# Combined weight quarters on GpSimd's own queue, ScalarE's queue first at the start, and S3/S4 formed where they are used

## The reference

```
c   = conv1d(x, weight[128, 32, 9], 4 groups, padding 4) + cond @ c_weight^T + bias     # [32, 128, 2048]
y   = c @ W[2048, 2048] + ffn_bias
d   = B_eff @ (A_eff @ c) + B_shared @ (A_shared @ c)    # rank 32 each; A_eff, B_eff mixed by gate per 4 samples
out = x + y + d
```

## Time and profile before

| | |
|---|---|
| median of 3 runs | 1772.81 us (1769.04 to 1773.53) |
| profiled execution | 1771.03 us, span 1769.2 us |
| busy: PE / PE weight loads / DVE / ACT / POOL | 1732.3 / 1482.9 / 996.0 / 668.0 / 184.7 us |
| DMA | 411.22 MB, mean 232 GB/s, nearly all on SP's queue |
| mean granted TensorE clock | 0.987 of full speed |

### The profile page before, as it was taken

How to read it: one execution, slowest core, us unless ns; L and a number is a source line. 1 busy time by engine, 2 the same in 40 slices (tenths; PEclk the granted TensorE clock), 3 DMA queues, 4 the chain that set the end, 5 groups by cost and what they waited for, 6 DMA issues and landing times.

```text
span 1769.2 us, 21998 instructions
## 1 busy us (share of the span) xinstructions
PE 1732.3 (98%) x8710; PEld 1482.9 (84%) x8710; DVE 996.0 (56%) x1183; ACT 668.0 (38%) x841; POOL 184.7 (10%) x70
## 2 busy tenths in 40 slices
PE   7999998999999998999999999999999999999998
PEld 7988887888788887999999888888888888888887
DVE  7566554552544489999997423345555544553332
ACT  6556655663322266565553212132322311121110
POOL 0023344000000012332223100000000000000000
PEclk9799999999999999999999999999999999999999
DMA  8668898643765646877776554457767798886654
GB/s 244 164 221 282 314 313 288 217 133 106 234 235 201 221 167 249 305 278 273 276 265 229 202 183 176 173 189 246 235 215 228 248 341 312 300 284 214 193 196 147
DMA packets 182287, 411.22 MB, mean 232 GB/s; under 512 B 58724, under 2 KB 94404, under 8 KB 177544
## 3 DMA queue, kind: packets, MB, share of 16 engines
q1 hardware_dynamic: 182040, 408.76, 68.2%
q10 hardware_dynamic: 144, 1.05, 0.2%
HBM read 263.72 MB, written 146.03 MB: 232 GB/s over the span
## 4 chain that ended last, share of the span: by engine, by line
PE 83%; DMA 7%; DVE 4%; POOL 3%; SPq 1%; issue 1%; ACT 1%; DVEq 0%; ACTq 0%
PE acc L1288 62%; PE cps L1204 13%; PE acc L1220 3%; DMA T<-g 3%; PE cps L1236 3%; DMA g<-in_L_ffn_kernel 2%; DVE x_q L893 1%; PE acc L1267 1%; POOL g L654 1%; POOL g L652 1%; POOL g L651 1%; POOL g L656 1%; DMA mixed_B<-b_raw 1%; DVE x_lo L900 1%; PE cps L1249 1%
## 5 line engine op out<-in xcount | busy, mean ns | idle before, releaser
L1288 PE MATMUL acc<-w_hi,y_t 128*128 128x512 f32 x3584 | 996.1, 392 | 0.0
L1288 PEld LDWEIGHTS acc<-w_hi,y_t 128*128 128x128 f32 x3584 | 667.2, 189 | 135.3 <-issue 1.6
L1288 PE MATMUL acc<-w_lo,y_t 128*128 128x512 f32 x1792 | 554.2, 390 | 0.0
L1288 PEld LDWEIGHTS acc<-w_lo,y_t 128*128 128x128 f32 x1792 | 337.6, 188 | 71.7
L684 ACT COPY x_q<-x_raw 32x512 f32<-32x512 f32 x248 | 268.7, 1084 | 50.1 <-DVE x_lo L900 38.6
L1204 PE MATMUL cps<-cw_hi,x_hi 128*128 128x384 f32 (+2 forms) x768 | 232.7, 303 | 10.5 <-DVE x_lo L900 6.9
L1204 PE MATMUL cps<-cw_lo,x_hi 128*128 128x384 f32 (+2 forms) x768 | 232.2, 302 | 0.0
L1204 PE MATMUL cps<-cw_hi,x_lo 128*128 128x384 f32 (+2 forms) x768 | 231.5, 301 | 0.0
L710 ACT CAST y_t<-g 128x1024 fp32r<-128x1024 f32 x96 | 101.1, 1053 | 335.0 <-PE acc L1288 309.3
L986 DVE TENSOR_TENSOR g<-acc,g 128x1024 f32<-128x1024 f32 x96 | 117.1, 1221 | 171.7 <-PE acc L1220 117.0
L947 DVE TENSOR_TENSOR y_t<-g,y_t 128x1024 fp32r<-128x1024 f32 x96 | 119.5, 1245 | 129.3 <-ACT y_t L710 129.2
(11 more groups left out here) (100 smaller groups left out, 1076.4 us busy)
## 6 DMA issues: line engine op xcount, KB each, us to landing
g<-U SPq DMA_DIRECT2D x80, 512.0 KB, 5.8
g<-A SPq DMA_DIRECT2D x64, 512.0 KB, 5.1
g<-in_x SPq DMA_DIRECT2D x64, 512.0 KB, 6.2
out<-g SPq DMA_DIRECT2D x64, 512.0 KB, 3.4
x_raw<-in_x SPq DMA_DIRECT2D x31, 1024.0 KB, 6.8
A<-g SPq DMA_DIRECT2D x48, 512.0 KB, 5.8
S<-g SPq DMA_DIRECT2D x48, 512.0 KB, 3.0
U<-g SPq DMA_DIRECT2D x48, 512.0 KB, 3.8
```

The source lines that it names most:

```text
L1288: ins = T.matmul(acc[:, b, m, :], y_buf[b][:, c, part, :], wt[:, k % SLOTS, m * 512:(m + 1) * 512], start=(c == 0 and part == 0 and wt is ...
```

## The change

- Forming: the four loads and four stores of each quarter chunk are issued by GpSimd itself, between its operations; SP's `forming` goes. SP still waits for all of it (`form_out`) before `load_y(16)`.
- Start: conv weights, x[0] and the first four B11 chunks are issued by ScalarE, in this order. VectorE forms cw_lo before the ctx copies and ctx_sum after `split_0(2)`; TensorE's ctx matmul stands behind conv(0)'s first group.
- Bias rows: split by `bias_hi` / `bias_lo` in iterations 15 and 80 and no longer in `b_split`.
- S3, S4: GpSimd forms nothing in phase 2. Phase 2 stores A21, A22, S1, S2 and loads A11 (double buffered); `difference(u)` on VectorE forms S3 = A11 - A21 and S4 = A12 - S2 in phases 3 and 6 from two loads (`load_y`, `load_other` into x_raw), one unit ahead.

```diff
@@ SP
-            def load_forming(j): ...
-            def store_formed(j): ...
-            def forming(u): ...
@@ load_y
-                elif f == 3:
-                    sp.wait_ge(s_out[1], 16 * (NP if p < 2 else p + 1))
-                    if p < 2:
-                        sp.wait_ge(s_out[2], 16 * NP)
+                elif f == 3 and p < 2:
+                    sp.wait_ge(s2_ready, NP - 1 + p)
-                src = {1: A12_d, 3: S3_d, 4: A22_d, 5: S1_d, 6: S4_d}[f]
+                src = {1: A12_d, 3: A11_d, 4: A22_d, 5: S1_d, 6: A12_d}[f]
+            def load_other(u):
+                f, p, b = u // NP, u % NP, u % 2
+                if f == 3:
+                    sp.wait_ge(yc_out[0], 16 * (NP + p + 1))
...
+                if diff_index(u) >= 2:
+                    sp.wait_ge(diff_ready, diff_index(u) - 1)
+                sp.dma_start(other[b], (A21_d if f == 3 else S2_d)[p]).then_inc(other_in[b], 16)
@@ load_sums -> load_a11
-                for i, src in enumerate((A11_d, A12_d)):
-                    if p == 0:
-                        sp.wait_ge(yc_out[i], 16 * NP)
-                        sp.wait_ge(y_lo_ready, 2 * NP)
-                    else:
-                        sp.wait_ge(s_out[1 + i], 16 * p)
-                    sp.dma_start(g[:, 2 + i], src[p]).then_inc(a1_in[i], 16)
+                if p < 2:
+                    sp.wait_ge(yc_out[0], 16 * NP)
+                    sp.wait_ge(y_lo_ready, 2 * NP - 1 + p)
+                else:
+                    sp.wait_ge(s2_ready, p - 1)
+                sp.dma_start(a11_buf[p % 2], A11_d[p]).then_inc(a1_in[p % 2], 16)
@@ GpSimd
             for j in range(NCH):
+                if j == 0:
+                    pool.wait_ge(la_used, RK)
+                else:
+                    pool.wait_ge(form_out, 64 * j)
+                for i, quarter in enumerate((B11, B12, B21, B22)):
+                    V.dma_start(g[:, 2 + i], quarter[j]).then_inc(form_in, 16)
                 pool.wait_ge(form_in, 64 * (j + 1))
                 V.tensor_tensor(g[:, 5], g[:, 5], g[:, 3], ALU.subtract).then_inc(form_done, 1)
                 V.tensor_tensor(g[:, 3], g[:, 3], g[:, 2], ALU.subtract).then_inc(form_done, 1)
                 pool.wait_ge(form_done, 4 * j + 2)
+                V.dma_start(T7_d[j], g[:, 5]).then_inc(form_out, 16)
                 V.tensor_tensor(g[:, 2], g[:, 5], g[:, 2], ALU.add).then_inc(form_done, 1)
+                V.dma_start(T5_d[j], g[:, 3]).then_inc(form_out, 16)
                 pool.wait_ge(form_done, 4 * j + 3)
+                V.dma_start(T6_d[j], g[:, 2]).then_inc(form_out, 16)
                 V.tensor_tensor(g[:, 4], g[:, 4], g[:, 2], ALU.subtract).then_inc(form_done, 1)
-            for p in range(NP):
-                pool.wait_ge(y_evac, 4 * (NP + p + 1))
-                pool.wait_ge(s2_ready, p + 1)
-                V.tensor_tensor(g[:, 2], g[:, 2], g[:, 0], ALU.subtract).then_inc(s3_ready, 1)
-                pool.wait_ge(a1_in[1], 16 * (p + 1))
-                V.tensor_tensor(g[:, 3], g[:, 3], s2_buf, ALU.subtract).then_inc(s4_ready, 1)
+                pool.wait_ge(form_done, 4 * j + 4)
+                V.dma_start(T4_d[j], g[:, 4]).then_inc(form_out, 16)
@@ ScalarE
+            act.dma_start(b_raw[:, 0:GC * TAPS], conv_w.rearrange("o i k -> o (i k)")).then_inc(conv_w_in, 16)
             act.dma_start(x_raw[:], x[0]).then_inc(x_in, 16)
+            for c in range(4):
+                act.dma_start(st[:, c], B11[c]).then_inc(t_in[c], 16)
...
+                if u in (NP - 1, 5 * NP):
+                    bias_hi(0 if u == NP - 1 else 1)
@@ VectorE
                 if p >= 1:
-                    dve.wait_ge(s4_ready, p)
+                    dve.wait_ge(s_out[1], 16 * p)
                     dve.wait_ge(y_lo_ready, u)
+            def difference(u):
+                b = u % 2
+                dve.wait_ge(y_in[b], 16 * (y_index(u) // 2 + 1))
+                dve.wait_ge(other_in[b], 16 * (diff_index(u) // 2 + 1))
+                V.tensor_tensor(y_in_buf[b], y_in_buf[b], other[b], ALU.subtract).then_inc(diff_ready, 1)
...
+                if u + 1 < NU and (u + 1) // NP in (3, 6):
+                    difference(u + 1)
                 if pf in (2, 3):
                     evac(pu)
```

More of the change, by code:

```diff
@@ L123, in build @@
         u2_buf = [g[:, b] for b in range(2)]
+        other = [x_raw[:, b * HALF:(b + 1) * HALF] for b in range(2)]
+        a11_buf = [g[:, 2 + b] for b in range(2)]
         s1_buf = g[:, 4]
@@ L224, in build @@
         s2_ready = sem("s2_ready")
-        s3_ready = sem("s3_ready")
-        s4_ready = sem("s4_ready")
-        s_out = [sem(f"s_out{i}") for i in range(3)]
+        other_in = [sem("other_in0"), sem("other_in1")]
+        diff_ready = sem("diff_ready")
+        s_out = [sem("s_out0"), sem("s_out1")]
         y_in = [sem("y_in0"), sem("y_in1")]
@@ L485, in store_y @@
                 sp.wait_ge(y_evac, 4 * (v + 1))
[L486 to L492, removed]
+                for i, dst in enumerate((A11_d, A12_d) if v < NP else (A21_d, A22_d)):
+                    sp.dma_start(dst[v % NP], g[:, i]).then_inc(yc_out[i], 16)
             sp.dma_start(cw_raw, c_weight).then_inc(small_in, 16)
@@ L543, in _ @@
                         load_y(w)
+                    if w < NU and w // NP in (3, 6):
+                        load_other(w)
                 if f in (2, 3):
@@ L589, in _ @@
                 if u + 1 in range(2 * NP, 3 * NP):
[L590 removed]
+                    load_a11(u + 1)
                 if early(pu):
@@ L730, in b_split, with bias_hi @@
                 A.copy(b_hi[:], b_raw[:]).then_inc(b_hi_ready, 1)
[L731 to L737, removed]
+            def bias_hi(half):
+                act.wait_ge(bias_in, 32 * (half + 1))
+                if half == 0:
+                    act.wait_ge(btwo_zero, 1)
+                else:
+                    act.wait_ge(lora_done, 2 * NP)
+                A.copy(b_two[R2:R2 + 1, :], x_raw[R2:R2 + 1, 0:HALF])
+                A.copy(b_two[R2 + RANK:R2 + RANK + 1, :], x_raw[R2 + RANK:R2 + RANK + 1, 0:HALF]).then_inc(bias_hi_ready, 1)
             def rearrange_0(i, rows):
@@ L964, in b_split, with bias_lo @@
                                 ).then_inc(b_lo_ready, 1)
[L965 to L968, removed]
-                                    ).then_inc(bias_ready, 1)
+            def bias_lo(half):
+                dve.wait_ge(bias_hi_ready, half + 1)
+                row = slice(R2 + RANK, R2 + RANK + 1)
+                V.tensor_tensor(b_two[row, :], x_raw[row, 0:HALF], b_two[row, :].bitcast(F32), ALU.subtract
+                                ).then_inc(bias_ready, 1)
             def pre_add(u):
@@ L1040, in _ @@
                                 ).then_inc(cw_lo_ready, 1)
-            dve.wait_ge(ctx_done, 1)
-            V.tensor_tensor(ctx_sum, acc[0:NS, 1, 0, 0:CH], bias_bc, ALU.add).then_inc(ctx_ready, 1)
             def rearrange_0(i, rows):
@@ L1077, in _ @@
             split_0(2)
+            dve.wait_ge(ctx_done, 1)
+            V.tensor_tensor(ctx_sum, acc[0:NS, 1, 0, 0:CH], bias_bc, ALU.add).then_inc(ctx_ready, 1)
             split_0(3)
@@ L1207, in conv @@
                     ins.then_inc(conv_done, 1)
+                    if v == 0 and i == 0:
+                        pe.wait_ge(ctxt_ready, 2)
+                        T.matmul(acc[0:NS, 1, 0, 0:CH], condT, cwT, start=True, stop=True).then_inc(ctx_done, 1)
             def lora(u):
@@ L1322, in _ @@
             T.matmul(acc[:, 0, 1, 0:NB], gate_exp, ident[0:NB, 0:NB], start=True, stop=True).then_inc(gcol_done, 1)
-            pe.wait_ge(ctxt_ready, 2)
-            T.matmul(acc[0:NS, 1, 0, 0:CH], condT, cwT, start=True, stop=True).then_inc(ctx_done, 1)
             pe.wait_ge(as_raw_in, 16)
```

74 lines of the change are left out of this document (34 added, 40 removed).

## The result

The changed kernel takes 1756.07 us (median of 6 runs, 1749.80 to 1758.39) against 1770.97 for the kernel before (6 runs, 1767.22 to 1773.53): ratio 0.9919, 95% interval 0.9905 to 0.9934. That is 14.9 us faster. The forecast was 1747, so the sign and the range held, and not much over half of the forecast gain came.

The account below looks back on a forecast made before the run. TensorE was busy 1732.3 of 1769.2 us, so only its waits and slow-clock stretches could be gained. Terms -12.6 - 1.3 - 2.2 - 0.8 - 9.0 = -25.9 gave 1745.1, as a median about 1747 us, range 1738 to 1762.

Parts of the forecast that it names:

- SP freed: Phase 0: with forming off SP, lora_B and mixed_B are issued early; permute waits and half-rate stretches go, -14.2 us.
- Collisions: Phase 0: GpSimd's operations and VectorE's copies hinder each other; none to eight collisions, 0 to 8.8 us, taken as +2.0.
- First round: Phase 0: first quarter loads start when mix_A(3) is done, beside the small mixed_A packets, +0.7 us (0 to 2.4).
- rival A: Phase 0 keeps a loss: rounds hit the copies every time, or mixed_B's packets land late; 1757 us, chance 0.14.
- Start: Start: conv(0) begins at 13.5 instead of 16.60, passed on only partly to product(0), -1.3 us (-3 to +2).
- Bias: Bias rows made earlier remove TensorE's waits of 2.4 us and 0.8 us (entry of phase 5): -2.2 and -0.8.
- Phase 2's entry: Without GpSimd's S3 and S4, the x_lo wait and the slow convolution behind it go, -9.0 us (-2.2 to -9.5).
- Phases 3 and 6: One more 512 KB load and VectorE subtraction per unit fit in: 0, at most 0.1 us a unit (+3.2).
- Rivals B and D: B: at phase 2's entry T load or ScalarE's order holds, 1754, 0.13; D: change doesn't do what it says, 1772, 0.03.
- Rival C: Forming becomes slow and blocks SP before load_y(16); at 49 us a round 1813 us, chance 0.08.

Follow-up runs that it names:

- e2: Changed kernel with the four forming operations on VectorE at the end of eight units, transfers still on GpSimd's queue: 1741.17 us (0.9843).
- e7: e2 with forming's loads and stores on SP's queue, VectorE forming in units 2 to 9: 1754.09 us (0.9908).
- e10: e2 plus four unused GpSimd subtractions on two real quarters, begun with the x_q copies, in four units of phase 0: 1745.35 us (0.9867).
- e9: e7 plus four unused GpSimd operations on the broadcast identity, forced onto the x_q copies in eight units of phase 0: 1753.25 us (0.9919).
- e12: Changed kernel with GpSimd's first round of operations held until VectorE has split mixed_A (a_parts): 1744.46 us (0.9870).
- e5: e2 with the old start (conv weights first on SP's queue, cw_lo after the ctx copies, ctx's matmul before conv(0)): 1744.40 us (0.9855).
- e6: e2 with the bias rows split at the entry of phases 1 and 5, as before the change: 1745.43 us (0.9861).
- e4: Kernel before the change with only S3 and S4 formed on VectorE in phases 3 and 6: 1761.14 us (0.9953).
- e8: e2 plus two unused GpSimd subtractions in each unit of phase 2, where S3 and S4 were formed before: 1748.46 us (0.9880).
- e3: Changed kernel with forming's loads and stores back on SP's queue, GpSimd still forming: 1755.17 us (0.9921).
- e11: e10 with two GpSimd subtractions instead of four in each of the four units: 1740.93 us (0.9838).
- e1: Changed kernel without GpSimd's four forming operations a round, the same transfers kept, T4 to T7 holding plain quarters: 1743.61 us (0.9855).

## Why the prediction was half right

By its own steps, forecast against the marks of the trace and the experiments:

- **SP freed, -14.2: right.** In e2, where nothing else is in the way, every unit from the second is 23.34 us; the 14.2 and the first hit's 1.24 are gone. e7 shows that it takes the move off SP's queue.
- **Collisions, "I take +2.0": the step that failed.** They cost 11.6. Position: none to eight was my range; five rounds met the copies (7.30, 14.72, 9.08, 14.67 and 14.74 us), and three of them cost something. Price: "a full collision costs TensorE 1.1 us; a unit has room for the rest of it" is true of copies of 13.3 us (e10: 1.0), and I carried it over to a kernel in which the hit is longer. The new kernel puts its store issues between the operations: four of them last from 185.05 to 197.03, where before they ran back to back from 111.52 to 122.09. That gives copies of 14.7. And it is not their length that is paid but their end: in each hit TensorE's wait is the time from the unit's mark to the end of the copies, less 14.42 us, and nothing where they end sooner. The three hits end 16.54, 17.63 (begun one w_lo split, 1.21 us, later) and 16.89 behind their marks and wait 2.13, 3.20 and 2.47; the hit before ended 15.52 behind and waited 1.09, the one of e10 15.15 and 0.73. So a late 9.67 in e9, ending 14.66 behind its mark, made TensorE wait 0.24, and 12.62 in e12, ending 14.45 behind, only 0.03. And I priced the wait alone, though I had seen in the earlier trace rows what follows a wait: 3.8 us at the lower clock. My bound of 8.8 for all eight was therefore too low.
- **First round, "+0.7 (0 to 2.4)": failed too.** It cost 5.8. I had looked for small packets in its way; it was GpSimd again, beside x_lo (4.81 for 2.39) and a_parts (2.69 for 0.42) in the one unit where ax_part wants a_parts at once. e12 takes 5.7 of it back.
- **Together** phase 0 was -12.6 in the forecast and is +2.0 by the marks (5.8 + 11.6 - 15.4). This is rival A's mechanism, with three hard hits instead of "every time", at its price of 1757; I gave it 0.14. The forecast's own range of 1740 to 1752 missed; the stated range held because it had been widened to take A in.
- **Start, -1.3:** 2.6 by mix_B, 2.5 by product(0) over all profiles, 3.2 by e5's median and 2.1 by its ratio. ctx_d's store, issued at 19.59, let the load behind it go at 21.00, 1.4 us where I took 2.7, and conv(0) began at 14.26.
- **Bias, -3.0:** both waits are gone, and e6 brings back 2.6 us of waits and 3.2 us by the ratios. **Phase 2's entry, -9.0:** 8.0 by e4 against before, 7.3 by e8, 8.9 by the marks (11.3 - 2.4). **Phases 3 and 6, 0:** no wait there. Rivals B and D are out: x_lo's chain was the cause (e8).
- **Rival C** had no part: rounds last about 31 us (I said 29) and the last store goes out at 322.55, far from 400. An issue on GpSimd takes 0.53 to 0.89 us, also beside the copies. The Trainium skill (SBUF — State Buffer, section A bandwidth-pool intuition that's wrong) has about 0.6 us alone and 3.1 beside a VectorE copy for a GpSimd DMA. These are figures of that section, not of the "DVE blocks DMA" box, and of a whole DMA; I had priced an issue by them. The issues are near the first, and none of the 64 comes near the second. The lock rule of the same page (Who interferes with whom: whoever comes first has the shared pair for the whole instruction, the other blocks) agrees with the single copies, one of which stood through each operation.

The two causes hide each other, which is why neither alone shows in the total:

| operations by | transfers on SP | on GpSimd's queue |
|---|---|---|
| GpSimd | 1755.2 (e3) | 1756.1 (the change) |
| VectorE | 1754.1 (e7) | 1741.2 (e2) |

Each edit alone is worth about 1 us or nothing, both together 14. Left open: the changed kernel's runs spread over 8.6 us and e12's over 14.6, where e2's spread over 3.6. Rounds that fall on the copies more or less hard from run to run would do that; only one run of each was profiled, so it isn't shown.

## What to carry to other kernels

When a long job moves off an in-order queue, ask what then sets its rhythm: here it went from "in step with the units" to a free-running 31 us beside 23.34, and its operations met another engine's work at every phase. Price a collision by where its end falls against the next deadline, not by its length or an earlier collision's cost: before the deadline it is free, behind it is paid us for us, and a wait can add slow clock on top. Put work that on GpSimd would hold up VectorE on VectorE itself if it is short there (four operations of 1.2 us in a gap of 5.4 us), and let the other engine move the data.

## What the runs showed of the hardware that I had not expected

- An operation on two real quarters holds one of VectorE's copies. Four of them stretch four of the eight copies: to 2.70, 2.70, 3.32 and 3.52 us with store issues between the operations (14.72 in all), to 2.7 each back to back in e10 (13.32 in all) and before. Two in e11 stretch two, to 2.7 (9.1 in all). The subtraction 14.72 - 9.96 = 4.76 is no rule: back to back, in e10, the operations take 10.70 us of the 13.32, and 2.62 is left. Operations that read a broadcast of the identity (e9) stretch three or four copies to 2.2 us, 4.8 to 6.5 us in all. Beside GpSimd's DMA issues alone (e2) eight copies take 4.9 us at most.
- A 512 KB store of T lands in 4.0 us (median) in the change and 3.9 in e2, from GpSimd's queue, and in 8.0 (e7) to 8.8 (before) from SP's. The queue is not the whole reason: in e1 GpSimd issues its four stores back to back, and they land in 8.4. What the reason is, no run here shows. A 512 KB load takes 6.7 (e1) to 8.5 us from GpSimd's queue and 5.0 from SP's. An issue takes 0.5 to 0.6 us on GpSimd and 0.3 to 0.5 on SP (medians; the 3.97 us of four in e7 hold the waits between them). The rows of the change, 100 to 330 us:
```profile
T<-g POOLq DMA_DIRECT2D x29, 512.0 KB, 4.0
g<-in_L_ffn_kernel POOLq DMA_DIRECT2D x28, 512.0 KB, 8.5
```
- A wait of 2.13 us was followed by a full clock (1.00 in 200 to 206), waits of 2.47 and 3.20 by 0.72: 0.2 against 1.8 us beyond the wait. The four waits of e10, 0.7 to 1.0 us, cost 0.2 beyond the wait each as well.
